# Other decay groups, and another order behind them, in the recurrence of a gated linear attention

## The reference

```python
q = x @ Wq.T                          # 16 columns
k_sig = sigmoid(x @ Wk.T)             # 16 columns
q = silu(q) * 16 ** -0.5
gf = log_sigmoid(-k_sig)
# over the tokens t, with a state S of 16 x 256:
#   S = exp(gf_t)[:, None] * S + k_t[:, None] * x_t[None, :];  o_t = q_t @ S
o = gla(q, k_sig, x, gf)
go = o @ Wog.T + x @ Wig.T
rms = o * rsqrt(mean(o * o, -1) + 1e-5) * g_weight
return rms * go * sigmoid(go)
```

## Time and profile before

| | |
|---|---|
| median of the runs | 983.83 us |
| profiled execution, its own time | 985.32 us |
| its span, first to last instruction | 983.6 us |
| busy in the span: TensorE, VectorE, ScalarE, GpSimd | 87%, 71%, 55%, 41% |
| mean granted clock of TensorE | 0.949 of full speed |
| from 600 to 760 us, in the recurrence stage: TensorE, VectorE, ScalarE, GpSimd | 124.45, 139.97, 99.38, 137.95 us of 160 |
| granted clock there | 0.91 |

### The profile page before, as it was taken

How to read it: one execution, slowest core, us unless ns; L and a number is a source line. 1 busy time by engine, 2 the same in 40 slices (tenths; PEclk the granted TensorE clock), 3 DMA queues, 4 the chain that set the end, 5 groups by cost and what they waited for, 6 DMA issues and landing times.

```text
span 983.6 us, 21335 instructions
## 1 busy us (share of the span) xinstructions
PE 857.0 (87%) x7188; PEld 720.6 (73%) x7188; DVE 695.4 (71%) x1317; ACT 545.3 (55%) x1064; POOL 402.2 (41%) x464
## 2 busy tenths in 40 slices
PE   4599999999999997799999987777777569999997
PEld 3367667777667764688888977777776458888887
DVE  7566777777777774477676668988888636677765
ACT  3146454454545545566666666666666346666674
POOL 3822222222222234232322225889998642333320
PEclk9679999999999998899999998899999769999999
DMA  5755666566664532100000000000000000000001
GB/s 174 95 78 78 129 99 89 76 100 85 96 94 72 83 56 41 34 2 1 1 0 1 1 1 1 1 0 0 0 0 1 1 1 22 24 21 21 22 23 43
DMA packets 33751, 40.99 MB, mean 42 GB/s; under 512 B 4319, under 2 KB 25216, under 8 KB 33648
## 3 DMA queue, kind: packets, MB, share of 16 engines
q1 hardware_dynamic: 33690, 40.20, 24.3%
HBM read 9.25 MB, written 5.24 MB: 15 GB/s over the span
## 4 chain that ended last, share of the span: by engine, by line
PE 41%; DVE 25%; ACT 14%; issue 12%; DMA 2%; SPq 2%; POOL 2%; DVEq 1%; ACTq 1%; POOLq 0%
DVE inter L1765 5%; PE bank L406 5%; PE pair_a L834 5%; PE bank L407 4%; PE bank L408 4%; ACT stk L1383 4%; ACT gact L1388 4%; PE pair_b L815 3%; PE bank L848 3%; PE pair_b L807 3%; PE bank L1034 3%; DVE spline L1832 3%; DVE am_lo L1851 2%; PE bank L1044 2%; DVE in_lo L1770 2%
## 5 line engine op out<-in xcount | busy, mean ns | idle before, releaser
L581 POOL TENSOR_SCALAR_AFFINE_SELECT prob<-prob 128x512 f32<-128x512 f32 x128 | 82.2, 642 | 223.2 <-ACT prob L1259 223.2
L1259 ACT ACTIVATE prob<-pair_a 128x768 f32<-128x768 f32 x128 | 103.7, 810 | 98.3 <-PE pair_a L834 97.2
L406 PE MATMUL bank<-wd_hi,in_hi 128*128 128x256 f32 x512 | 147.7, 289 | 8.0 <-DVE X L1776 6.5
L1770 DVE TENSOR_TENSOR in_lo<-inter,in_hi 128x512 fp32r<-128x512 f32 x128 | 98.7, 771 | 78.8 <-ACT in_hi L1396 78.2
L408 PE MATMUL bank<-wd_hi,in_lo 128*128 128x256 f32 x512 | 142.9, 279 | 0.0
L407 PE MATMUL bank<-wd_lo,in_hi 128*128 128x256 f32 x512 | 142.8, 279 | 0.0
L1612 DVE TENSOR_REDUCE mx<-pair_b 128x6 f32<-128x768 f32 x124 | 118.0, 952 | 33.1 <-PE pair_b L815 32.5
L1396 ACT ACTIVATE in_hi<-inter 128x512 fp32r<-128x512 f32 x128 | 80.9, 632 | 94.6 <-DVE inter L1765 94.6
L1765 DVE TENSOR_TENSOR inter<-gact,pair_b 128x512 f32<-128x512 f32 x128 | 87.6, 684 | 48.8 <-ACT gact L1388 48.7
L406 PEld LDWEIGHTS bank<-wd_hi,in_hi 128*128 128x128 f32 x512 | 97.1, 190 | 16.2 <-issue 5.7
L407 PEld LDWEIGHTS bank<-wd_lo,in_hi 128*128 128x128 f32 x512 | 97.5, 191 | 3.6
(11 more groups left out here) (242 smaller groups left out, 2360.6 us busy)
## 6 DMA issues: line engine op xcount, KB each, us to landing
stack<-stage SPq DMA_DIRECT2D x192, 128.0 KB, 4.7
result<-X SPq DMA_DIRECT2D x8, 512.0 KB, 2.9
X<-in_attn_a_x SPq DMA_DIRECT2D x14, 256.0 KB, 5.0
stack<-mrow SPq DMA_DIRECT2D x128, 4.0 KB
wdx<-spline SPq DMA_DIRECT2D x1, 1024.0 KB
wd_lo<-wdx SPq DMA_DIRECT2D x16, 64.0 KB
spline<-factor_basis SPq DMA_DIRECT2D x1, 1008.0 KB, 7.1
win<-decay_windows SPq DMA_DIRECT2D x1, 672.0 KB, 7.3
```

The costliest lines, as they stand in the source:

```text
L406: pe.matmul(dst, l_hi, r_hi, start=first, stop=False)
L1259: act.activation(prob[:, p % 4], pair_a[:, :, P:4 * P], ACT.Exp, scale=DK ** -0.5).then_inc(a_e, 1)
L1770: dve.tensor_tensor(in_lo[:, m % LAG, :], inter[:, m % 2, :], in_hi[:, m % LAG, :].bitcast(F32), ALU.subtract).then_inc(f_.il, 1)
```

## The change

The seven decay groups become five, at rows 0, 16, 32, 64 and 96 of 112; the rows between are zero. Groups 0 to 2 are the borders at 64, 192 and 128. The two near groups hold the 64-token blocks, one the first halves and one the second halves of both 128-token blocks. The product is made in three pieces of 128 keys by 128 queries: keys 0 and queries 0 over all 112 rows, keys 0 and queries 1 over the first 48 rows, keys 1 and queries 1 over all. The fourth piece, which the mask made zero, is not computed, and the masked products are 384 columns instead of 512.

The window multiplications on GpSimd go. The decays are written by ScalarE in three pieces which leave the zeros of `dec` alone (set once), and the scans read them and a table of starts. The reciprocal is made in two pieces. The key's factor 16 ** -0.5 moves into ScalarE's affine copy. In the streams of ScalarE and VectorE the values' high and low parts go ahead of those of queries and keys, the turned x goes ahead of the squares, and the mean square is VectorE's last step.

```diff
-NG = 7
-GR = NG * KG
+GROUPS = (0, 16, 32, 64, 96)
+CROSS = 48
+NEAR = (64, 96)
+GR = 112
+AM = 3 * P
...
+def decay_starts():
+    w = np.zeros((GR, 2, S), np.float32)
+    for g, ref in ((0, 64), (1, 192), (2, 128)):
+        r = slice(KG * g, KG * g + KG)
+        w[r, 0, ref] = 1.0
+        w[r, 1, ref - 1] = 1.0
+    for h in range(2):
+        w[NEAR[h]:NEAR[h] + KG, 0, 64 * h::P] = GROW
+    return w
...
 # GpSimd
-            def g_windows(n):
...
-                    if nxt:
-                        g_windows(n + 1)
...
-            pool.memset(dk[:, S - 1:S], 0.0).then_inc(s_gc, 1)
+            pool.memset(dec, 0.0).then_inc(s_gc, 1)
+            pool.memset(fk, 0.0).then_inc(s_gc, 1)
...
 # TensorE, g_products
-                for t in range(TB):
-                    keys = slice(P * t, P * t + P)
-                    i = mm3(pe, pair_a[:, 0, S * t:S * t + S], qk_hi[:, 1, keys], qk_lo[:, 1, keys],
-                            qk_hi[:, 0, :], qk_lo[:, 0, :], True, True)
+                for at, rows, k, q in ((0, GR, 0, 0), (P, CROSS, 0, 1), (2 * P, GR, 1, 1)):
+                    k, q = slice(P * k, P * k + P), slice(P * q, P * q + P)
+                    i = mm3(pe, pair_a[:, 0, at:at + P], qk_hi[0:rows, 1, k], qk_lo[0:rows, 1, k],
+                            qk_hi[0:rows, 0, q], qk_lo[0:rows, 0, q], True, True)
...
 # ScalarE, g_activate
-                act.wait_ge(g_.w, upto(g_.w, n - 1, 4))
+                act.wait_ge(g_.kd, upto(g_.kd, n - 1, 1))
...
-                act.activation(dec, dt, ACT.Copy, bias=0.5, scale=-0.5).then_inc(g_.de, 1)
+                for rows, cut in (((0, 32), P), ((32, CROSS), 0), ((NEAR[0], GR), 64)):
+                    to, of = dec[rows[0]:rows[1]], dt[rows[0]:rows[1]]
+                    if cut:
+                        to, of = (v.rearrange("p (w s) -> p w s", s=cut)[:, :, 1:] for v in (to, of))
+                    i = act.activation(to, of, ACT.Copy, bias=0.5, scale=-0.5)
+                i.then_inc(g_.de, 1)
...
 # ScalarE, period
                     if nxt:
                         g_activate(n + 1)
+                    if nxt:
+                        g_high_values(n + 1, 1 - u)
                     if cur:
                         g_high_qk(n)
+                    if nxt2:
+                        g_high_turned(n + 2, u)
                     if prev:
                         g_squares(n - 1, 1 - u)
                     if nxt:
                         g_high_x(n + 1, 1 - u)
-                        g_high_values(n + 1, 1 - u)
-                    if nxt2:
-                        g_high_turned(n + 2, u)
...
 # VectorE, g_scans and g_decayed
-                dve.wait_ge(g_.w, upto(g_.w, n, 4))
-                dve.wait_ge(g_.qd, upto(g_.qd, n - 1, 1))
-                dve.tensor_tensor_scan(fq, dq, win[:, 1], 0.0, ALU.mult, ALU.add).then_inc(g_.sf, 1)
-                dve.tensor_tensor_scan(fk[64:GR, ::-1], dk[64:GR, ::-1], win[64:GR, 3, ::-1], 0.0, ALU.mult,
-                                       ALU.add).then_inc(g_.sb, 1)
+                dve.wait_ge(g_.de, upto(g_.de, n, 1))
+                dve.wait_ge(g_.kd, upto(g_.kd, n - 1, 1))
+                dve.tensor_tensor_scan(fq, dec, win[:, 0], 0.0, ALU.mult, ALU.add).then_inc(g_.sf, 1)
+                dve.tensor_tensor_scan(fk[0:CROSS, S - 2::-1], win[0:CROSS, 1, S - 2::-1], dec[0:CROSS, S - 1:0:-1],
+                                       0.0, ALU.add, ALU.mult).then_inc(g_.sb, 1)
...
-                dve.reciprocal(fk[0:64], fq[0:64]).then_inc(g_.rc, 1)
+                for h in range(2):
+                    near = slice(NEAR[h], NEAR[h] + KG)
+                    f, t = (v[near].rearrange("p (t h s) -> p h t s", h=2, s=64)[:, h] for v in (fk, fq))
+                    i = dve.reciprocal(f, t)
+                i.then_inc(g_.rc, 1)
...
-                dve.tensor_tensor(qk[:, 0], qwn, fq, ALU.mult).then_inc(g_.qd, 1)
+                dve.tensor_tensor(qk[:, 0], qs, fq, ALU.mult).then_inc(g_.qd, 1)
...
-                dve.tensor_tensor(qk[:, 1], kwn, fk, ALU.mult).then_inc(g_.kd, 1)
+                dve.tensor_tensor(qk[:, 1], ks, fk, ALU.mult).then_inc(g_.kd, 1)
...
 # VectorE, period
                     if cur:
                         g_decayed(n)
+                    if nxt:
+                        g_low_values(n + 1, 1 - u)
+                    if cur:
                         g_low_qk(n)
+                    if nxt2:
+                        g_low_turned(n + 2, u)
                     if prev:
                         g_mean_square(n - 1)
-                    if nxt:
-                        g_low_values(n + 1, 1 - u)
-                    if nxt2:
-                        g_low_turned(n + 2, u)
```

More of the change, by code:

```diff
@@ L124, in spline_features @@
             np.ascontiguousarray(moments.astype(np.float32)))
-def decay_windows():
-    w = np.zeros((GR, 6, S), np.float32)
-    run, start, krun, kstart, qwin, kwin = (w[:, n] for n in range(6))
-    for g in range(4):
+def decay_starts():
+    w = np.zeros((GR, 2, S), np.float32)
+    for g, ref in ((0, 64), (1, 192), (2, 128)):
         r = slice(KG * g, KG * g + KG)
-        run[r] = 1.0
-        run[r, ::64] = 0.0
-        start[r, ::64] = GROW
-        qwin[r, 64 * g:64 * g + 64] = 1.0
-        kwin[r, 64 * g:64 * g + 64] = KG ** -0.5
-    for g, ref, length in ((4, 64, 64), (5, 192, 64), (6, 128, 128)):
-        r = slice(KG * g, KG * g + KG)
-        run[r, ref + 1:ref + length] = 1.0
-        start[r, ref] = 1.0
-        krun[r, ref - length:ref] = 1.0
-        kstart[r, ref] = 1.0
-        qwin[r, ref:ref + length] = 1.0
-        kwin[r, ref - length:ref] = KG ** -0.5
+        w[r, 0, ref] = 1.0
+        w[r, 1, ref - 1] = 1.0
+    for h in range(2):
+        w[NEAR[h]:NEAR[h] + KG, 0, 64 * h::P] = GROW
     return w
 def build(nc, x, a_wq, a_wk, a_wv, a_wo, b_wq, b_wk, b_wog, b_wig, g_weight, cpw_in, psi_in, feat_in, mom_in,
-          windows, out):
+          starts, out):
     outer = ExitStack()
@@ L275, in build @@
         qk = gwork(2, GR)
-        qs, kt, ks, dt, dec, qwn, kwn, dq, dk, fq, fk = (gwork(1, GR)[:, 0] for _ in range(11))
+        am = am.rearrange("p t k -> p (t k)")[:, 0:AM]
+        qs, kt, ks, dt, dec, fq, fk = (gwork(1, GR)[:, 0] for _ in range(7))
         wdx = nc.dram_tensor("wdx", [INTER + 1, D], F32, kind="Internal").ap()
@@ L1231, in _ @@
             turned = prep_bank[6][:, 0:4 * KG].rearrange("p (m k) -> p m k", k=KG)
-            for g in range(NG):
-                act.activation(wqk_hi[:, :, :, KG * g:KG * g + KG].rearrange("p n c k -> p (n c) k"), turned,
+            for g in GROUPS:
+                act.activation(wqk_hi[:, :, :, g:g + KG].rearrange("p n c k -> p (n c) k"), turned,
                                ACT.Copy).then_inc(s_prep_hi, 1)
@@ L1584, in low_gla_weights @@
             def low_gla_weights():
-                dve.wait_ge(s_prep_hi, 6 + NG)
+                dve.wait_ge(s_prep_hi, 6 + len(GROUPS))
                 turned = prep_bank[6][:, 0:4 * KG].rearrange("p (m k) -> p m k", k=KG)
-                for g in range(NG):
-                    cols = slice(KG * g, KG * g + KG)
+                for part in (wqk_hi, wqk_lo):
+                    for gap in (CROSS, NEAR[0] + KG):
+                        dve.memset(part[:, :, :, gap:gap + KG].bitcast(F32), 0.0)
+                for g in GROUPS:
+                    cols = slice(g, g + KG)
                     i = dve.tensor_tensor(wqk_lo[:, :, :, cols].rearrange("p n c k -> p (n c) k"), turned,
```

57 lines of the change are left out of this document (24 added, 33 removed).

## The result

The changed kernel takes 1018.14 us (median of 4 runs, 1015.24 to 1019.74) beside 984.72 for the kernel before (4 runs, 983.77 to 985.68, on the same chip): a ratio of 1.0336, 95% interval 1.0305 to 1.0367. It is 33.4 us slower, where 971.3 was forecast. The profiled execution of it took 1019.66, with a span of 1018.0.

A forecast was written before the change was run, and what follows sets the result against it. VectorE, with its waits and turns with GpSimd, was taken to bound the recurrence stage; periods of 11.0 us save 12.0, with end terms 12.5 net, from 983.83 to 971.3 us. Its own range was 967 to 976, over all cases 957 to 986.5.

The forecast's parts named there:

- the one of ScalarE: ScalarE's queue: three decay activations for one, some 0.6 us more, covered by 3.48 us of idle time there.
- layout: One recurrence period from masking to masking: low part of products ends at 4.25, masking 6.78 later, period 11.0 us.
- for what I don't see: Chance of 0.12 left for an uncovered decay activation or TensorE at its lower clock in the output train, mostly slow.
- Reciprocals: VectorE: one of 1.74 us becomes two of 0.95; the pair costs 0.08 to 0.41 more, 0.41 taken.
- The hold of a change of partition group: VectorE: an instruction starting in another partition group waits for all before it; 0.11 us a step, at three reciprocal hand-overs.
- may go: VectorE's scans: two hand-over steps of 0.11 us may vanish, 0 to 0.22 gained, mostly 0 because they lie inside turns.
- The products: TensorE: nine products paid by the piece take 1.30 us against 0.97 for six; bounds 0.9 and 1.9.
- rival by columns: TensorE's products paid by their columns: nine take 0.9 us, period 10.6, kernel 967 us; chance 0.12.
- slow rival: Recurrence stage: GpSimd's low part of x precedes the forward scan, three turns, period 12.1, 985.2 to 986 us; chance 0.22.
- Three turns: The slow rival by its title: three VectorE turns behind GpSimd a period, if masking comes 0.03 us later; chance 0.22.
- VectorE keeps its turn: Short scan and low part of products go ahead of waiting GpSimd: period 9.2 to 9.7, 953 to 958 us; chance 0.12.
- if ScalarE's decays ... release VectorE: Sign that the prediction is wrong altogether: in the recurrence stage VectorE is released by ScalarE's decays; no size given.

The follow-up runs named there:

- wait alone: The kernel before, with ScalarE's activations of sample n+1 also waiting for the decayed keys of n: 1004.69 us, ratio 1.0199.
- two tiles: The changed kernel with two tiles each for activated queries, keys and decays, used in turns by samples: 972.87 us, ratio 0.9875.
- split and moved: Changed kernel, one tile each: activations' waits split, silu and keys' copy behind x's rounding, squares and mean square ahead of turned x: 965.3 us, ratio 0.9811.
- order alone: The kernel before with only the new order of ScalarE's and VectorE's queues; groups, windows and buffers as before: 991.68 us, ratio 1.0071.
- One multiplication less: The two tiles kernel without GpSimd's first residual multiplication, by g_weight, so the output lacks that factor: 962.63 us, ratio 0.9779.

## Why the prediction was wrong

**The step that failed** is the one of ScalarE: "That queue runs to about 5.6 in the layout and its next task, the high part of queries and keys, comes at 8.3. Before, it idles there for 3.48; without that cover it would cost 0.6." It takes for granted that the activations run where they ran. The wait in front of them had changed, from the window multiplications of the last sample, for which ScalarE never stood in the profile before, to its decayed keys, and those come at the end of the idle time, not ahead of it. The 3.48 were no cover but the place in front of the wait. Neither the sum nor a rival has it; that the multiplications go was costed as GpSimd's gain, and what else their semaphore did was not followed. The 0.12 "for what I don't see" name an uncovered decay activation, but the range, 957.0 to 986.5, was drawn over turns and products and held nothing of this size. The wait alone, set into the kernel before, costs 20.0 us; taken out of the change by second tiles, it gives 45.3 (1018.14 to 972.87); split and moved, 52.8, some of it by the other order behind it.

**The sum by its parts**, as means of the twelve middle periods, in us. "Low part" is that of the products in the first two columns and that of queries and keys behind them; the last column is the time that the products take on TensorE, inside the fourth (nine pieces, but six before and in the wait alone):

| | masking to end of low part | to end of decayed keys | to low part | to masking | period | products |
|---|---|---|---|---|---|---|
| layout | 4.25 | 4.00 | 0.70 | 2.08 | 11.03 | 1.30 |
| before | 4.45 | 3.53 | 0.70 | 3.26 | 11.95 | 0.97 |
| changed | 2.37 | 4.66 | 3.90 | 2.95 | 13.88 | 2.13 |
| two tiles | 2.90 | 4.62 | 0.93 | 2.61 | 11.06 | 1.71 |
| wait alone | 3.95 | 3.80 | 2.31 | 3.27 | 13.33 | 0.99 |

- From the end of the decayed keys to the low part of queries and keys: 3.20 more than laid out, all of it the queue behind the wait.
- Masking to the end of the low part of the products: 1.88 less. Two turns were laid out. The scans mostly had none, since GpSimd's work lies elsewhere in the longer period. The low part had none in any period (0.52 to 0.56), also where GpSimd was waiting: in the period shown above GpSimd's multiplication runs from 677.33 to 679.11, and ends 1.16 behind the low part.
- From there to the end of the decayed keys: 0.66 more. In the period above the decayed queries take 1.17 behind GpSimd, whose last residual instruction runs from 680.85 to 682.14. The prediction has such a turn in the last two periods only.
- From the start of the low part of queries and keys to masking: 0.87 more, nearly all of it the products. In the period above they run at full clock at first (granted 1.00) and at half of it for the last three (0.50), as the rows of TensorE in the kernel after show:

```profile
687.40 0.33 PE L400 MATMUL pair_a<-qk_hi 112*128 112x128 f32 x1 [3.95 <-DVE qk_lo L1834]
687.57 0.28 PE L401 MATMUL pair_a<-qk_lo,qk_hi 112*128 112x128 f32 x1
...
688.63 0.41 PE L401 MATMUL pair_a<-qk_lo,qk_hi 112*128 112x128 f32 x1
688.85 0.41 PE L402 MATMUL pair_a<-qk_hi,qk_lo 112*128 112x128 f32 x1
```

**The clock** has a price of its own. In the kernel after, nine products take 1.50 where all run at full clock and 2.55 where all run at half, and masking waits for them. Two neighbouring periods, alike in the other parts, show it (low part of queries and keys, then masking; granted clock 0.50 under the first products, 1.00 under the second):

```profile
630.57 0.69 DVE L1834 TENSOR_TENSOR qk_lo<-spline,qk_hi 112x512 fp32r<-112x512 f32 x1
...
633.91 0.56 DVE L1840 SCALAR_TENSOR_TENSOR spline<-pair_a,causal 128x384 f32<-128x384 f32 x1 [1.76 <-PE pair_a L402]
...
644.73 0.69 DVE L1834 TENSOR_TENSOR qk_lo<-spline,qk_hi 112x512 fp32r<-112x512 f32 x1
...
647.11 0.56 DVE L1840 SCALAR_TENSOR_TENSOR spline<-pair_a,causal 128x384 f32<-128x384 f32 x1 [0.79 <-PE pair_a L402]
```

The first of these periods takes 14.24, the second 13.20. With products of 2.13 in the mean, some 0.6 a period are the clock's, by an estimate from these rows 8 to 9 of the 33.4 us. It looks like a follower of the wait, for which TensorE stands too: from 600 to 760 the clock was granted at 0.91 before and 0.79 after, and 0.87 with two tiles, where TensorE waits less and eleven of sixteen groups of products take 1.45 to 1.52. No run changes the clock alone.

**What held.** Reciprocals: 0.947 each and 1.91 the pair, 0.95 forecast. The hold of a change of partition group: the pair starts 0.03 after its forerunner's end (679.32 behind 679.29), and the decayed queries 0.03 after the pair's (681.26 behind 681.23). From the last instruction of the statistics (L1801) to the decayed queries are 2.13 for 1.73 before, 0.40 more for the 0.41 forecast. At the scans the steps went, as "may go" had it: the short scan starts 0.08 before the forward scan's end (676.85 under 676.93) and the low part of the products 0.07 before the short scan's, since all of them now begin at partition 0. Masking 0.56 and the low part 0.52; the mean square 0.17. The decay pieces cost 1.24 for three, some 0.8 more than the one of 0.42 where 0.6 were said.

**The products** came out within the bounds, but the argument for them was a misreading. In the two-tile kernel nine at full clock start at 686.96 and the last ends at 688.47: 1.51, where 1.30 was said. The second and third of a group of three start 0.16 to 0.17 and 0.11 to 0.12 behind the one ahead, the next group 0.20. The 0.9 of the rival by columns was not met anywhere. But the "sixteen plain fp32 ones" of rows 6, from which the price by the piece was taken, are eight matmuls of the program (`moments` issues eight at a time) in two records each. They cost 0.23 a matmul and not 0.116, and say nothing of rounded ones. That 1.30 lay near was luck.

**The period of 11.0** was right as a mean in the kernel whose ScalarE does what the layout had it do (11.06 with two tiles and the new order), but not by its turns. There the periods run from 10.5 to 11.8. Of sixteen, seven have a long forward scan (1.25 to 1.80) and four a long short scan (1.70 to 1.72), one of them both, and all but three have a turn at the decayed queries (0.81 to 1.19). The layout had the forward scan free and turns at the short scan and the low part of the products; the low part has none in any period. One size in it explains the forward scan: GpSimd's power instruction was put at 0.93, by the row at the stage's end. The fifteen others of the kernel before take 0.69 to 0.72, and so do those of this kernel in the stage's middle, behind idle stretches of 1.86 to 3.75. So the low part of x asks 0.23 sooner, and in seven periods ahead of the scan, as in the first half of the slow rival; its second half, GpSimd's multiplication waiting when that scan ends, mostly didn't follow. That 972.87 agrees with 971.3 is therefore compensation, and luck: masking to the end of the low part takes 1.35 less than laid out, and the three other parts 0.62, 0.23 and 0.53 more.

**The rivals.** "Three turns" lies at 985 to 986 and doesn't tell 1018; its picture was met only with the old groups, in one period of the kernel before (622.19), one with the order alone and four with the wait alone. "VectorE keeps its turn" was right by half. Where a GpSimd instruction waits at the end of the short scan, the low part goes first in all 64 such cases of the runs with the new groups, and GpSimd in all 31 of those with the old ones. At the end of the forward scan it is GpSimd, in 24 of 25 cases with the new groups and in all 18 with the old. The low part saves about 1.0 a period by it, which the layout had as a turn. In the new groups both instructions start 0.07 to 0.09 before the end of the one ahead, so that alone doesn't decide it; what does is open. The line that warned, that all is wrong "if ScalarE's decays ... release VectorE", was near: it is ScalarE's rounding of the values, queued behind the decays, that releases VectorE. The line had no price.

**Still open** is what the new order would bring without turns. With one tile and the new groups it costs 8.1, with two tiles nothing that can be told, in the kernel before 7.0; the rows show turns in its way in the last case, but no run takes them away while keeping both orders comparable.

## What to carry to other kernels

For each instruction that a change removes, list who waited for it and what has to stand in for that wait; a step that looks like mere arithmetic may be the copy that frees a tile. Then lay the queue anew from the moment at which the new wait ends: all that is queued behind it on that engine is paid by the next one in the chain, and idle time that was seen before the change lies in front of that wait and covers nothing. When such a wait can't go, give each instruction only the wait that its own tile needs, put the needed roundings ahead of it (here a split and a move were as good as second tiles), and fill what VectorE waits with work that has time.

## What the runs showed of the hardware

- With VectorE and GpSimd taking turns, what counts is which GpSimd instruction waits when VectorE comes, not how much GpSimd does. One multiplication less (1.3 to 2.2 us) took a turn of 0.72 off VectorE in a period, and squares and mean square ahead of the turned x took away the long short scans and cut the longest forward scan from 1.80 to 1.25.
- A waiting GpSimd instruction did not always go first. Where the low part of the products started 0.07 before the end of the short scan (new groups), it ran in 0.52 and GpSimd ended 1.14 to 1.18 behind it; where it started 0.03 behind that end (old groups), GpSimd went first and the low part took 1.57 to 1.62.
- One VectorE instruction can stand behind several of GpSimd: a forward scan of 0.68 took 3.61 (635.07, the kernel with the order alone), and ended 0.55 behind the second of two GpSimd instructions that began after it.
- A small instruction of 2 elements took 0.17 alone and 0.41 in a turn before, and 0.70 in the kernel with the wait alone.
- Rounded-fp32 products of 128 columns and 112 or 48 rows follow one another in 0.11 to 0.20 at full clock, those of 256 columns in 0.12 (688.81, 688.93, 689.05 in the two-tile kernel): half the columns are not half the time. At the lower clock the last ones of the change stand 0.22 to 0.27 apart. A plain fp32 matmul of 128 columns shows as two records and takes 0.23 to 0.25 (eight in 2.02).
- GpSimd's power instruction of two elements a partition took 0.70 in most places and 0.88 to 1.08 in others. A pause ahead of it doesn't decide this: in the changed kernel it took 0.70 behind 5.05 of idle time, and 0.88 right behind the last residual instruction. Those of 0.88 to 0.91 in the kernels with the new groups all ended 0.23 or 0.24 behind VectorE's decayed keys, so they look like turns that VectorE had first; no run tests it.
